# Cross attention and a routed FFN on one core: block 0 reordered on TensorE and VectorE, the weights' slots computed on GpSimd

## The reference, cut to what matters

```
x = x + xattn(layernorm(x), ctx)            # 4 heads of 64 channels, twice (global, local)
xf = layernorm(x)                           # 2048 tokens x 256
logits = xf @ gate_w                        # 8 experts
top_w, top_idx = top_k(logits, 2); top_w = softmax(top_w)
h = gelu(xf @ w1[e] + b1[e])                # 256 -> 1024
y = h @ w2[e] + b2[e]                       # 1024 -> 256
x = x + sum over the two experts of top_w * y
```

## Time and profile before

| | us |
|---|---|
| median of 3 runs | 341.05 |
| lowest, highest | 340.5, 342.69 |
| the profiled execution, its time | 339.34 |
| the profiled execution, its span | 337.5 |
| PE busy | 308.4 (91%) |
| DVE busy | 255.8 (76%) |
| ACT busy | 234.6 (70%) |
| POOL busy | 173.1 (51%) |

### The profile page before, as it was taken

One profiled execution on the slowest core, in us unless ns is written; L12 is line 12 of the kernel. 1 busy time (PEld: TensorE's weight loads), 2 busy tenths in 40 slices (PEclk: granted clock), 3 DMA queues, 4 the chain that ended last, 5 costly groups with the idle time before them and its releaser, 6 DMA issues.

```text
span 337.5 us, 11901 instructions
## 1 busy us (share of the span) xinstructions
PE 308.4 (91%) x4073; PEld 285.6 (85%) x4073; DVE 255.8 (76%) x577; ACT 234.6 (70%) x537; POOL 173.1 (51%) x189
## 2 busy tenths in 40 slices
PE   7688898999779998999999999999999999999960
PEld 4678787998778897999999999999899999998950
DVE  8899998977879887787878778878778766656620
ACT  2599898982635887878778878778788665656530
POOL 6988989974142353544444444444444445443311
PEclk9999999999999999999999999999999999999996
DMA  7999999999610297788887977897878897888321
GB/s 250 292 337 349 320 380 372 322 395 361 240 35 18 53 294 205 231 221 261 210 264 202 277 204 236 236 272 200 249 227 234 241 249 225 234 242 235 86 31 16
DMA packets 49219, 78.56 MB, mean 233 GB/s; under 512 B 12117, under 2 KB 25625, under 8 KB 47114
## 3 DMA queue, kind: packets, MB, share of 16 engines
q1 hardware_dynamic: 39208, 66.72, 55.9%
q0 software_dynamic: 7600, 10.48, 20.1%
q10 hardware_dynamic: 2354, 0.59, 0.7%
HBM read 31.07 MB, written 9.64 MB: 121 GB/s over the span
## 4 chain that ended last, share of the span: by engine, by line
PE 68%; DMA 7%; issue 3%; DVE 3%; POOL 2%; SPq 1%; POOLq 1%; ACT 0%; DVEq 0%; ACTq 0%
PE bank L1212 29%; PE bank L1227 28%; DMA W<-in_w 3%; DMA shared<-xn_rows,row_of 3%; PE bank L1186 3%; PE bank L1086 1%; PE bank L1229 1%; DMA out<-shared,row_of 1%; PE bank L1045 1%; PE bank L1039 1%; PE bank L1061 1%; DVE W L958 1%; PE bank L1173 1%; PE bank L1104 1%; SPq L353 1%
## 5 line engine op out<-in xcount | busy, mean ns | idle before, releaser
L1227 PE MATMUL bank<-W,shared 128*128 (+1 forms) x936 | 108.5, 273 | 0.0
L1212 PE MATMUL bank<-shared,XR 128*128 128x128 f16 x1680 | 100.0, 218 | 1.9 <-issue 1.7
L1212 PEld LDWEIGHTS bank<-shared,XR 128*128 128x128 f16 x1680 | 96.7, 97 | 3.4 <-issue 2.9
L1227 PEld LDWEIGHTS bank<-W,shared 128*128 128x128 f16 x936 | 89.8, 98 | 9.9
L504 POOL DMA_INDIRECT out<-shared,row_of x39 | 61.8, 1584 | 51.2 <-ACT shared L656 24.8
L497 POOL DMA_INDIRECT shared<-xn_rows,row_of x39 | 40.6, 1042 | 89.9 <-DVE w_of L1020 72.9
L647 ACT ACTIVATE shared<-shared 128x512 f32<-128x512 f32 x78 | 49.1, 630 | 47.6 <-DVE shared L1004 37.4
L1024 DVE SCALAR_TENSOR_TENSOR shared<-shared,XP 128x512 f16<-128x512 f32 x70 | 52.4, 749 | 25.9 <-ACT shared L649 15.8
L1004 DVE SCALAR_TENSOR_TENSOR shared<-bank,XP 128x512 f32<-128x512 f32 x70 | 52.5, 750 | 20.9 <-PE bank L1212 12.3
L649 ACT ACTIVATE shared<-shared,XP 128x512 f16<-128x512 f32 x70 | 50.6, 723 | 2.3
L958 DVE SCALAR_TENSOR_TENSOR W<-W,wscale (+1 forms) x32 | 40.9, 1281 | 1.9 <-issue 1.2
(11 more groups left out here) (171 smaller groups left out, 388.8 us busy)
## 6 DMA issues: line engine op xcount, KB each, us to landing
XR<-W SPq DMA_DIRECT2D x140, 256.0 KB
W<-in_w SPq DMA_DIRECT2D x16, 1024.0 KB, 8.4
shared<-in_ctx_t SPq DMA_DIRECT2D x16, 256.0 KB, 5.7
W<-in_ctx SPq DMA_DIRECT2D x16, 128.0 KB, 7.4
out<-XR SPq DMA_DIRECT2D x16, 128.0 KB, 7.1
xn_rows<-W SPq DMA_DIRECT2D x16, 128.0 KB, 7.1
XR<-in_x SPq DMA_DIRECT2D x3, 512.0 KB, 6.1
shared<-xn_rows,row_of POOLq DMA_INDIRECT x39
```

The costliest lines, as they stand in the source:

```text
L1212: mm = pe.matmul(pHT[n][m][:, f % 4, :], first[:, c, w, f * P:(f + 1) * P], XT[:, n, v, c, :], start=(c == 0 and w == 0 and v == 0), stop= ...
L1227: pe.matmul(pY[n], hT[:, n, v, f, :], whole(Wh[:, slot, at:at + D]), start=(f == 0 and w == 0 and v == 0), stop=False)
```

## The change: what it does

1. **Fillers.** Behind the squares of experts 4, 5, 6 of the second layer come 14 fillers each (10 before). Behind those of expert 7 come none (22 before), so the table's products follow at once.
2. **Register load.** VectorE's load of the expert's number stands between the one-hot matrices and the wait for the table, no longer behind the scales of the second layer's weights. The three other operations that stood in that place, and one beside them, leave VectorE.
3. **Slots.** `slots_of_blocks()` runs on GpSimd, between gather 2 and gather 3, in 20 operations instead of 8 on VectorE. A sum over an axis becomes adds in halves, and the comparison is written once for each of 7 ranks.
4. **Order of VectorE.** `low` of piece 2 comes before the low half of block 1's `XT` (where the slots were), `low` of piece 3 behind block 0's first `hb`.
5. **Order of TensorE.** The two banks of block 0's first layer are cleared by two products of zeros, ahead of 36 fillers (40 before). Block 0's products then run in three passes of 16: high weights by high rows, low weights by high rows, and, behind block 1's transposes, high weights by low rows.

```
@@ VectorE
-            chain(dve.tensor_tensor(ends[:, :], offs[:, :], cnt_blk[:, :], ALU.add))
-            beside(dve.tensor_tensor(step_e[:, 0:E - 1], permf[:, 1:E], permf[:, 0:E - 1], ALU.subtract))
-            chain(dve.tensor_tensor(eqm, eqr, row(ends[:, :]), ALU.mult))
-            chain(dve.tensor_reduce(endr[:, :], eqm, AX.X, ALU.add))
-
+            held = {"src": bass.ds(dve.value_load(perm[0:1, 1:2], min_val=0, max_val=E - 1), 1)}
             dve.wait_ge(table_mm, N2)
...
                 if i == -1:
-                    slots_of_blocks()
+                    dve.wait_ge(high_ok, 3)
+                    low(2, held["src"], spare_slot, wscale[:, 1, held["src"]])
...
                         if m == 0 and i == 0:
-                            dve.wait_ge(high_ok, 3)
-                            low(2, held["src"], spare_slot, wscale[:, 1, held["src"]])
+                            dve.wait_ge(high_ok, 4)
+                            low(3, held["src"], spare_slot, wscale[:, 1, held["src"]])
...
-                        if m == 0 and i == 0:
-                            dve.wait_ge(high_ok, 4)
-                            low(3, held["src"], spare_slot, wscale[:, 1, held["src"]])
@@ GpSimd
             for i in range(-2, NB + 2):
                 b = i + 2
+                if i == 1:
+                    slots_of_blocks()
...
+                for j in range(E - 1):
+                    pool.tensor_scalar(planes[:, j, :], iotaB128[:, :], endr[:, j:j + 1], None, ALU.is_ge).then_inc(slot_step, 1)
+                pool.wait_ge(slot_step, 13)
+                pool.tensor_tensor(planes, planes, step_e[:, 0:E - 1].rearrange("p (j o) -> p j o", o=1)
+                                   .broadcast_to([P, E - 1, NB]), ALU.mult).then_inc(slot_step, 1)
@@ TensorE
                 squares_of_second(e)
-                keep_busy(pIdle, 10)
-            keep_busy(pIdle, 12)
+                if e < E - 1:
+                    keep_busy(pIdle, 14)
...
+            def first_of_block_0():
+
+
+                first = Wh[:, SPARE, 0:4 * PIECE].rearrange("p (c r f) -> p c r f", c=C, r=2)
+                pe.wait_ge(high_ok, 2)
+                pe.wait_ge(xh_ok, 1)
+                for w in range(2):
+                    if w == 1:
+                        pe.wait_ge(low_ok, 2)
+                    for f in range(FC):
+                        for c in range(C):
+                            pe.matmul(pHT[0][f // 4][:, f % 4, :], first[:, c, w, f * P:(f + 1) * P], XT[:, 0, 0, c, :],
+                                      start=False, stop=False)
+                fetched_turned(1)
```

More of the change, by code:

```diff
@@ L491, in _, with slots_of_blocks @@
             pool.wait_ge(x1_out, 16 * T)
+            def slots_of_blocks():
+                planes = crossed.rearrange("p b j -> p (b j)").rearrange("p (j b) -> p j b", j=E - 1)
+                pool.wait_ge(perm_ok, 1)
+                pool.tensor_tensor(step_e[:, 0:E - 1], permf[:, 1:E], permf[:, 0:E - 1], ALU.subtract).then_inc(slot_step, 1)
+                pool.tensor_tensor(ends[:, :], key[:, :], iotaE[:, :], ALU.add).then_inc(slot_step, 1)
+                pool.wait_ge(slot_step, 2)
+                pool.tensor_tensor(ends[:, :], offs[:, :], ends[:, :], ALU.add).then_inc(ends_ok, 1)
+                pool.wait_ge(ends_ok, 1)
+                pool.tensor_tensor(eqm, eqr, ends.rearrange("p (o e) -> p o e", o=1).broadcast_to([P, E, E]), ALU.mult)\
+                    .then_inc(slot_step, 1)
+                for n, w in ((3, 4), (4, 2)):
+                    pool.wait_ge(slot_step, n)
+                    pool.tensor_tensor(eqm[:, :, 0:w], eqm[:, :, 0:w], eqm[:, :, w:2 * w], ALU.add).then_inc(slot_step, 1)
+                pool.wait_ge(slot_step, 5)
+                pool.tensor_tensor(endr[:, :], eqm[:, :, 0], eqm[:, :, 1], ALU.add).then_inc(slot_step, 1)
+                pool.wait_ge(slot_step, 6)
+                for j in range(E - 1):
[3 more added lines that the diff above has]
+                                   .broadcast_to([P, E - 1, NB]), ALU.mult).then_inc(slot_step, 1)
+                pool.wait_ge(slot_step, 14)
+                pool.tensor_tensor(planes[:, 0:3, :], planes[:, 0:3, :], planes[:, 3:6, :], ALU.add).then_inc(slot_step, 1)
+                pool.wait_ge(slot_step, 15)
+                pool.tensor_tensor(planes[:, 0, :], planes[:, 0, :], planes[:, 1, :], ALU.add).then_inc(slot_step, 1)
+                pool.tensor_tensor(planes[:, 2, :], planes[:, 2, :], planes[:, 6, :], ALU.add).then_inc(slot_step, 1)
+                pool.wait_ge(slot_step, 17)
+                pool.tensor_tensor(slot_of[:, :], planes[:, 0, :], planes[:, 2, :], ALU.add).then_inc(slot_step, 1)
+                pool.wait_ge(slot_step, 18)
+                pool.tensor_scalar(wslot[:, :], slot_of[:, :], float(SPARE), None, ALU.add).then_inc(wslot_ok, 1)
@@ L966, in _ @@
                 low(n, held["src"], spare_slot, wscale[:, 0, held["src"]])
[L968 to L977, removed]
             for i in range(-1, NB + 1):
@@ L1177, in _, with fetched_turned @@
                     pe.matmul(pSum[:, 2 * E:], ones32[:, :], wsq[:, 2 * E:], start=True, stop=True).then_inc(wsum2_mm, 1)
-            keep_busy(pIdle, 40)
+            for m in range(2):
+                pe.matmul(ps[m][:, :], ones3[32:64, :], ones[32:64, 0:1].broadcast_to([32, 512]), start=True, stop=False)
+            keep_busy(pIdle, 36)
+            def fetched_turned(b):
+                pe.wait_ge(xg_ok[b % 3], 16 * (b // 3 + 1))
+                after(pe, gts_ok, b)
+                for c in range(C):
+                    mm = pe.transpose(pGT[:, c, :], XG[:, b % 3, c * P:(c + 1) * P], ident[:, :])
+                mm.then_inc(gt_ok, 1)
+            def first_of_block_0():
[6 more added lines that the diff above has]
+                    for f in range(FC):
+                        for c in range(C):
+                            pe.matmul(pHT[0][f // 4][:, f % 4, :], first[:, c, w, f * P:(f + 1) * P], XT[:, 0, 0, c, :],
+                                      start=False, stop=False)
+                fetched_turned(1)
+                for f in range(FC):
+                    for c in range(C):
+                        mm = pe.matmul(pHT[0][f // 4][:, f % 4, :], first[:, c, 0, f * P:(f + 1) * P], XT[:, 0, 1, c, :],
+                                       start=False, stop=(f % 4 == 3 and c == C - 1))
+                    if f % 4 == 3:
+                        mm.then_inc(h_ok, 1)
             for i in range(-1, NB + 1):
                 b = i + 1
[L1182 to L1187, removed]
+                if b < NB and b != 1:
+                    fetched_turned(b)
                     if b == 0:
@@ L1197, in _ @@
                 b = i
-                if 0 <= b < NB:
+                if b == 0:
+                    first_of_block_0()
+                elif 0 < b < NB:
                     n = b % 2
```

2 lines of the change are left out of this document (1 added, 1 removed).

## The result

| | before | after |
|---|---|---|
| median of 20 runs, us | 341.16 | 344.17 |
| ratio, 95% interval | | 1.0079 (1.0054 to 1.0104) |
| the profiled execution, its time (span) | 339.34 (337.5) | 344.87 (343.1) |
| mean granted clock | 0.991 | 0.975 |
| block 5's first layer starts | 130.13 | 135.16 |

The change makes the kernel slower, by 2.7 us on the ratio: within 1%, as forecast. The range ended at 343.9: the median lies 0.3 above that, while the ratio applied to the 341.05 from which the forecast started gives 343.7, just inside. A kernel now and then has an execution that is some per cent longer whatever the change (363.17 was one of after's 20), and the ratios are taken without these. The profiled execution of before was 1.8 under its median, that of after 0.7 above, so the two traces lie 5.5 apart where the medians lie 3.0 apart.

What follows compares the result with a forecast made beforehand. PE's products bound 140 to 320 us, waits on gathers the first blocks. 0.9 won earlier and gather 3 late made block 5's first layer 1.1 later: span 338.6, time 340.4, plus 1.71 to the median, 342.2; range 339.6 to 343.9.

Steps and rivals of the forecast that it cites:

- table end 95.2: Table products on TensorE: without fillers ahead of them the last ends at 95.2 instead of 96.1, 0.9 us earlier.
- The gain of 0.5 forecast for `hb` and `w_of`: Block 0 on VectorE: `hb` at 103.2 instead of 103.74, `w_of` at 105.8 instead of 106.33.
- The 0.9 that was put on parts 1, 2, 4 and 5 together: Everything but the slots' move: block 5's first layer 0.5 to 1.2 us earlier, taken as 0.9.
- The slots' price: The 20 slot operations on a free GpSimd, waits between them included: 6.5 us, with 5.2 and 7.5 as ends.
- The lock: GpSimd waits for any running VectorE operation with two SBUF tensor inputs; 5.9 us of room, so 6.5 do not fit.
- Gather 3: Queued behind the slots on GpSimd: issue ends at 111.9 to 112.5, lands at 113.8 to 114.4 instead of 111.04.
- Gather 6's wait and the 1.20 behind it: Ahead of block 5's first layer: 5.02 and 1.20 us before, not added on top, since PE is then later.
- TensorE's gap: Ahead of block 3's transposes TensorE stands still from about 110.2, for about 4 us.
- (C): Rival: the gap lowers TensorE's clock, costing 2.1 us on top of the late gather, 343.8 to 345.7; chance 0.08.
- (A): The forecast: slots make gather 3 late, slower by 0.6 to 2.5 us, range 341.6 to 343.6; chance 0.44.
- (B): Rival: the slots on GpSimd are done in time, 0.5 to 1.2 us won, 339.85 to 340.55; chance 0.38.
- (D): Rival: gain and late gather cancel, within 0.5 of 341.05, slots done near 109.5; chance 0.10.

Runs made afterwards that it cites:

- e6: The kernel before with only the filler change behind the second layer's squares (14 behind experts 4 to 6, none behind 7): 338.41 us, ratio 0.9954.
- e5: The kernel of e1 with the fillers behind the second layer's squares as before (10 behind each, 12 more behind the last): 339.44 us, ratio 0.996.
- e1: The changed kernel with the slots back on VectorE, so that GpSimd issues gather 3 directly: 338.95 us, ratio 0.9961 of before.
- e4: The changed kernel with five VectorE operations beside the slots reading their second tensor from PSUM, values not right: 339.00 us, ratio 0.9975 of before.
- e3: The changed kernel with 64 fillers in TensorE's gap ahead of block 3's transposes: 342.84 us, ratio 1.0051 of before.
- e12: The kernel of e3 timed once more: 343.67 us, ratio 1.0084 of before.
- e10: The changed kernel with 64 fillers ahead of block 3's transposes and before's fillers behind the second layer's squares: 346.13 us, ratio 1.0149 of before.
- e9: The changed kernel itself, timed again beside e10: 344.27 us, ratio 1.0073 of before.

## Why the prediction was right, and where its sizes were off

- **Part 1, table end 95.2, 0.9 won.** The one-hot matrices came 0.8 later in this execution. Counted from their start the table's last product ended after 96.24 - 92.72 = 3.5, before after 96.12 - 91.91 = 4.2: 0.7 won. In the time, e6 gave 1.6 with an interval that holds 0.9; but e5, with the 22 fillers back in, is as fast as e1 without them, so the timed runs do not show that part 1 is worth 0.9 beside the other parts. "The other fillers change only a wait for W2" missed that without the 22 the clock falls to 0.63 right behind the table. That cost next to nothing only since 36 fillers were there to take it.
- **Part 2.** The 0.86 before `low` is gone, `low` started at 98.09 (97.2 + 0.8 expected). In the time: nothing that can be told.
- **Parts 4 and 5.** The three passes took what was forecast (32 products in 1.97, 16 in 1.07). Block 1's transposes came at 103.11, 1.2 later than before, 0.8 of it this execution's. The gain of 0.5 forecast for `hb` and `w_of` did not come in full: they began at 104.29 and 106.92, against 103.74 and 106.33 before, so with 0.8 taken off 0.25 and 0.2 were won. The wait of 1.72 that was to hide the clearing products was used up by the slow fillers. The 0.9 that was put on parts 1, 2, 4 and 5 together was measured as 1.3 (e1).
- **The slots' price, 6.5 on a free GpSimd: 7.2 (e4).** The eight operations with a scalar came to 2.9, not 2.4: the seven comparisons took 0.36 each, not 0.30, which had been guessed from a row of one element per partition.
- **The lock, the step that decides the sign: right.** 10.6 us in place of 7.2, through exactly the operations named. The Trainium skill (SBUF — State Buffer, Who interferes with whom) says that a VectorE instruction with two SBUF inputs contends with a GpSimd instruction that reads SBUF, and that the shared ports are an exclusive lock; its sentence that whoever issues first keeps them for the whole instruction stands there with VectorE's 2-port modes. This trace agrees with it for two inputs as well: L498 of 8 elements started inside a `low` of 1.28 and ended 0.05 behind it.
- **Gather 3.** Its issue began at 112.37 and ended at 113.44, forecast 111.9 to 112.5 for the end: 0.9 behind the later of the two, of which 0.8 is this execution's later start. Landing at 115.3, forecast 113.8 to 114.4. Gather 6's wait and the 1.20 behind it are gone, as forecast. Block 5's first layer was forecast for 131.8 at the latest and began at 135.16: 0.9 of the 3.4 is gather 3, 2.4 the clock.
- **TensorE's gap, "about 4": 3.96.** And here a second case came true beside the forecast: (C), with 0.08. I had put it apart from (A) as a rival, though (A) itself produces the gap that (C) needs. Together they were put at 343.8 to 345.7, where 344.17 lies. The chance of (C) given (A) should have been even or better, for the only rows on the question, the 42 products at 109 ns after idleness, spoke for it. That row was not read quite right: the 42 did not come from no work at all (four products of TensorE began at 2.27 and took 3.75, just ahead of them), and the granted clock reads 1.00 there, so the 1.2 GHz was taken from their duration alone. The 2.1 borrowed from it was near the 2.4 measured, with more luck than reason.
- **Size of the whole.** Forecast +1.1, measured +2.7: the direction and the way to it were right, and that the time ended at the edge of the range and not beyond it owes something to the width given to (A). In the profiled pair the missing term is the clock, 2.4, which the forecast itself left out. After's other executions point the same way: four of its 20 took 340.5 to 341.1, at mean granted clocks of 0.977 to 0.984, and the fifteen from 342.1 to 346.0 had 0.972 to 0.976. Against it stands that filling the gap gave back only 0.4 on the mean of e3 and e12, with an uncertainty of about 1.3, and that e10 shows a late gather followed by further waits. So the loss by the slots (4.0 against e1, 3.5 against e4) is shown (uncertainty about 1.3), and its division between a late gather, a slow clock and later waits is shown for single executions only.
- **(B) and (D)** fell: the slots ended at 112.10, not by 109.5. In the chances, the top of (A) was counted among the ways to be 3.4 slower, but its own range ends at 2.5.
- **A version that beats both.** Part 1 alone (338.41), parts 1 and 2 (339.25), all but part 3 (338.95), or all but 1 and 3 (339.44): 0.9954 to 0.9961 of before, and not to be told apart.

## What to carry to other kernels

Before moving small operations to an idle GpSimd, list VectorE's operations with two SBUF tensors in that stretch and give GpSimd only the time between them; if the next gather's issue is queued behind, the slack must hold the stretched sum, not the free one. If a forecast contains a gap on TensorE longer than any in the trace, the slower clock behind it belongs in that forecast and not in a rival of its own. A profile of one execution hides how much a DMA's landing varies: fillers between such a landing and the next real product come on top in the late ones (96.96 against 96.24 for the table's end), though no timed run here shows a price for it (e5 against e1).

## What the runs showed of the hardware that was not expected

- The issue of an indirect DMA on GpSimd is stretched beside a two-input VectorE operation, as the prediction had read from a 1.92: 1.71 at 98.51 in after, 1.70 in e1, 0.95 alone.
- TensorE was busy for 3.53 of 4.00 us in 92 to 96 of after, with the table's products (39 columns each) most of it, and the granted clock still fell to 0.63 in the 4 us behind, where it was busy all the time. With 22 products of 128 columns ahead of the table it stayed at 1.00 in before and e5, and fell to 0.62 in e10.
- Behind 3.96 us without work the granted clock was 0.50 from 116 to 120 (after), behind 3.88 the same (e9); behind 1.06 it was 1.00 (e4).
- Gather 3 landed 2.9 to 3.0 after its issue's start in after, e3, e4, e9 and e12, and 4.4 after it in e10, with the same bytes; gather 6 took 5.02 in before, where the DMA engines were busier (share 0.93 from 123 to 129, against 0.18 in after from 112 to 115).
